# Three layer norm roots per row: from ScalarE's square root to GpSimd's power

## The reference, cut to what matters

```python
def _layernorm(x, axis=-1, eps=1e-05):
    m = jnp.mean(x, axis=axis, keepdims=True); v = jnp.var(x, axis=axis, keepdims=True)
    return (x - m) / jnp.sqrt(v + eps)
x = _layernorm(x + L0_attention(x))       # differential attention, 16 heads of 8
x = _layernorm(x + L0_ffn(x))             # gate, up, down with 4 bit blocks
x = _layernorm(x + L1_attention(x))       # 16 query heads, 4 key heads, causal
x = _layernorm(x + L1_ffn(x))             # eight experts, each token to one of them
```

## Time and profile before

| what | value |
|---|---|
| median of 3 runs (lowest, highest) | 1262.83 us (1258.26, 1266.27) |
| the profiled execution: its time, its span | 1266.14 us, 1264.3 us |
| mean granted TensorE clock in it | 0.843 of full |
| PE, DVE, ACT, POOL busy | 81%, 62%, 51%, 34% of the span |
| instructions | 20021 |

### The profile page before, as it was taken

How to read it: one execution, slowest core, us unless ns; L and a number is a source line. 1 busy time by engine, 2 the same in 40 slices (tenths; PEclk the granted TensorE clock), 3 DMA queues, 4 the chain that set the end, 5 groups by cost and what they waited for, 6 DMA issues and landing times.

```text
span 1264.3 us, 20021 instructions
## 1 busy us (share of the span) xinstructions
PE 1021.1 (81%) x7121; PEld 520.7 (41%) x7121; DVE 786.8 (62%) x1785; ACT 641.5 (51%) x1581; POOL 424.9 (34%) x512
## 2 busy tenths in 40 slices
PE   2588846889999878999988887999988847998754
PEld 1122321233455332455445442355444447455544
DVE  4789347983777678760787667862577562467431
ACT  1177612776266344677167434686257514257423
POOL 3000020300776304000776502200485630487411
PEclk7578955899999875799999775799999968999957
DMA  5300063000013000320103000230100005100052
GB/s 154 96 3 3 10 184 59 2 2 11 0 35 76 1 2 9 125 86 10 31 26 93 1 1 2 83 106 32 32 1 10 1 6 209 32 1 10 1 192 63
DMA packets 54305, 56.83 MB, mean 45 GB/s; under 512 B 13688, under 2 KB 46016, under 8 KB 53440
## 3 DMA queue, kind: packets, MB, share of 16 engines
q1 hardware_dynamic: 53184, 53.47, 14.3%
q0 software_dynamic: 1024, 2.10, 0.6%
HBM read 43.16 MB, written 16.20 MB: 47 GB/s over the span
## 4 chain that ended last, share of the span: by engine, by line
PE 50%; DVE 21%; ACT 10%; issue 8%; POOL 4%; DMA 4%; SPq 3%; POOLq 0%; ACTq 0%; DVEq 0%
PE ps L1583 8%; DVE mx L969 8%; PE ps L1566 5%; PE ps L1612 5%; PE ps L1625 5%; PE ps L1645 4%; PE ps L1655 4%; PE ps L1404 3%; PE ps L1500 3%; ACT PROB L1261 2%; PE ps L1415 2%; PE ps L1398 2%; PE ps L1541 2%; ACT PROB L1303 2%; DMA qst<-mrow 2%
## 5 line engine op out<-in xcount | busy, mean ns | idle before, releaser
L969 DVE TENSOR_REDUCE mx<-ps 128x1 f32<-128x512 f32 x512 | 323.7, 684 | 90.3 <-PE ps L1541 88.1
L1261 ACT ACTIVATE PROB<-ps 128x512 f32<-128x512 f32 x512 | 276.6, 602 | 166.1 <-PE ps L1566 164.4
L577 POOL TENSOR_SCALAR PROB<-PROB,rsum 128x128 f32<-128x128 f32 (+3 forms) x224 | 229.8, 1038 | 72.4 <-DVE rsum L1102 72.0
L1303 ACT ACTIVATE PROB<-ps,mx 128x128 f32<-128x128 f32 (+3 forms) x256 | 133.1, 527 | 165.6 <-DVE mx L1097 163.9
L1583 PE MATMUL ps<-PROB,v 128*32 128x256 f32 x2048 | 184.2, 452 | 3.0 <-ACT OREG L1270 2.6
L1541 PE MATMUL ps<-kst,qst 24*128 24x512 bf16 x512 | 158.9, 477 | 34.1 <-DVE mx L969 26.6
L1566 PE MATMUL ps<-qst,kst 27*128 27x512 bf16 x512 | 142.3, 450 | 39.3 <-ACT PROB L1261 22.8
L558 POOL CAST mparts<-mx 128x16 bf16<-128x16 f32 x32 | 7.0, 218 | 449.4 <-DVE mx L969 427.1
L1097 DVE TENSOR_REDUCE mx<-ps 128x1 f32<-128x128 f32 (+3 forms) x256 | 113.0, 483 | 64.4 <-PE ps L1628 64.2
L1645 PE MATMUL ps<-cst,PROB 128*128 128x128 f32 x640 | 114.2, 298 | 38.5 <-ACT PROB L1318 13.5
L1625 PE MATMUL ps<-MREG,QREG 64*128 64x384 f32 (+3 forms) x512 | 106.9, 495 | 0.0
(11 more groups left out here) (217 smaller groups left out, 1379.6 us busy)
## 6 DMA issues: line engine op xcount, KB each, us to landing
wexp<-expert_rows SPq DMA_DIRECT2D x44, 514.0 KB, 5.2
qk_terms<-RREG SPq DMA_DIRECT2D x48, 128.0 KB, 2.1
kst<-qk_terms SPq DMA_DIRECT2D x16, 192.0 KB
qst<-qk_terms SPq DMA_DIRECT2D x16, 192.0 KB
RREG<-sorted_x SPq DMA_DIRECT2D x4, 704.0 KB, 4.7
sorted_y<-RREG SPq DMA_DIRECT2D x4, 704.0 KB, 3.9
expert_rows<-in_L_ffn_W_dram SPq DMA_DIRECT2D x1, 2048.0 KB
expert_rows<-in_L_ffn_W_dram SPq DMA_DIRECT2D x4, 512.0 KB
```

What stands on the lines that cost most here:

```text
L577: pool.tensor_scalar(tile, tile, rsum1[:, 2 * v + half:2 * v + half + 1], None, ALU.mult).then_inc(scaled1, 1)
L969: dve.tensor_reduce(mx0[:, ga % 2, col:col + 1], ps[:, max_bank(k, MAX_SLOT[n]), :], AX, ALU.max, negate=True).then_inc(slot0_free, 1)
L1261: act.activation(prob0[:, s % 2, q % 4, q % 8 // 4], ps[:, s0_banks[q % len(s0_banks)], :], ACT.Exp, scale=float(HD0) ** -0.5).then_inc(ex ...
L1303: act.activation(prob1[:, half, at:at + w], ps[:, a1_bank(v, half), 0:w], ACT.Exp, bias=mx1[:, col:col + 1], accum_out=sum1[:, col:col + 1 ...
```

## The change

The second, third and fourth root of a row leave ACT. POOL adds the epsilon and raises the sum to the power -0.5 (a `tensor_tensor` with a 128x4 tile filled with -0.5), which gives the reciprocal root at once. POOL also makes `var2`. So ACT loses three square roots a row, DVE loses three reciprocals and the two products of `both_scales`, and POOL gains two operations (`root_b`) and seven (`roots_c`), with new semaphores `rootB` and `rootC`. `roots_c` stands in POOL's list behind `max_parts0` of group 1 and ahead of that of group 2; `root_b` stands behind `max_parts0` of group 6. The first and the fifth root of a row stay on ACT, in `attention1`. No transfer is moved.

```diff
+            pool.memset(minus_half, -0.5).then_inc(setup_pool, 1)
...
+            def root_b(r):
+                pool.wait_ge(varB, 2 * r + 2)
+                step(pool.tensor_scalar(stB[:, 0], mvB[:, :, 1], LN_EPS, None, ALU.add)); settle()
+                pool.tensor_tensor(stB[:, 1], stB[:, 0], minus_half, ALU.pow).then_inc(rootB, 1)
+
+            def roots_c(i):
+                pool.wait_ge(varC, 2 * i + 1)
+                step(pool.tensor_scalar(stC[:, 0], mvC[:, :, 1], LN_EPS, None, ALU.add)); settle()
+                pool.tensor_tensor(stC[:, 1], stC[:, 0], minus_half, ALU.pow).then_inc(rootC, 1)
+                pool.wait_ge(rootC, 2 * i + 1)
+                step(pool.tensor_tensor(var2, mvC[:, :, 1], stC[:, 1], ALU.mult)); settle()
+                step(pool.tensor_tensor(var2, var2, stC[:, 1], ALU.mult)); settle()
+                step(pool.tensor_scalar(var2, var2, LN_EPS, None, ALU.add)); settle()
+                pool.tensor_tensor(inv2, var2, minus_half, ALU.pow).then_inc(rootC, 1)
...
                     if k < BATCH:
                         max_parts0(k, g)
+                    if 0 <= i and g == 1:
+                        roots_c(i)
+                    if hidden and g == 6:
+                        root_b(r)
...
-            def both_scales(i):
-                dve.wait_ge(stdC, 3 * i + 1)
-                step(dve.reciprocal(stC[:, 1], stC[:, 0])); settle()
-                step(dve.tensor_tensor(var2, mvC[:, :, 1], stC[:, 1], ALU.mult)); settle()
-                dve.tensor_tensor(var2, var2, stC[:, 1], ALU.mult).then_inc(varC, 1)
...
-                if (s, c) == (1, 2):
-                    both_scales(i)
                 if (s, c) == (1, 3):
+                    dve.wait_ge(rootC, 2 * i + 1)
...
                 if (s, c) == (2, 1):
-                    dve.wait_ge(stdC, 3 * i + 2)
-                    step(dve.reciprocal(inv2, stC[:, 0])); settle()
+                    dve.wait_ge(rootC, 2 * i + 2)
...
                 if (s, c) == (12, 1):
-                    scale(ZB, X, mvB, stB, stdB, 2 * r + 2, lnB)
+                    dve.wait_ge(rootB, r + 1)
...
-                if (s, c) == (1, 1):
-                    std_c(3 * i + 1)
-                    act.wait_ge(varC, 3 * i + 2)
-                    act.activation(stC[:, 0], var2, ACT.Sqrt, bias=eps[:, 0:1]).then_inc(stdC, 1)
...
-                if (s, c) == (11, 1):
-                    std_b(2 * r + 2)
```

## The result

The changed kernel took 1257.01 us (median of 22 runs, 1248.61 to 1264.69) against 1265.94 us for the kernel before (22 runs, 1258.26 to 1270.69); the ratio is 0.9938, 95% interval 0.9924 to 0.9953. By the ratio that is 7.9 us off, by the two medians 8.9; forecast were 13.2 us off and 1249.6 us. Where a run's ratio stands, the us off given with it are by the ratio too. In two later comparisons with a fresh set of runs of the kernel before the ratio was 0.9901 [0.9872, 0.9930] and 0.9928 [0.9906, 0.9949], 12.6 and 9.1 us off. So the direction holds and the size was too large, also over all three.

The account below looks back on a forecast made before the run. No engine is full; waits around the roots bound the kernel, ACT standing between exponentials. Terms 7.9 - 0.4 + 5.8 + 0.4 - 0.5 = 13.2 us off give 1249.6 us from the median; range 1240 to 1268, forecast's own 1243 to 1256.

Parts of the forecast that it names:

- The pair in overlaps 1 and 2: Second and third root: without ACT's wait and table loads DVE's next maxima start 3.94 us sooner per overlap, 7.9 us gained.
- the table loads stay: Rival: loads are put elsewhere and stay; only the wait for the second variance goes, 1.6 us twice; 1260 us, chance 0.04.
- The feed-forward root: In overlaps 1 and 2: 1.4 us from lost table loads and 1.5 us from the clock not falling, each; 5.8 us gained.
- Contention: POOL's power slows DVE's 128x704 scaling behind the pair's variances in overlaps 1 and 2; 0.2 us each, 0.4 us lost.
- Overlap(0) at 0: Feed-forward root of overlap(0): ACT's reload came after its wait for PE and delays no PE work, so 0 us gained.
- the maximum rows' transfers: Behind overlap(1)'s pair, transfers are wanted 3.9 us sooner, leaving 1.8 us to land; only more time would cut the gain.
- The late roots: Overlaps 3 and 4: 0.4 us gained from a table load in overlap(3), 0.5 us charged for POOL's chain in both.
- p: Time of one POOL power on 128x4, priced by no profile row; taken as 0.6 us, with ends 0.2 and 3.2 us.
- under 1 us: Sign to look for in the profile: POOL's powers take less than 1 us each by their spacing.
- half is given back: Rival: clock still falls at the feed-forward stretch and PE or DVE wait behind the pairs; 6.5 us less, 1256, chance 0.11.
- The clock rises sooner: Rival: behind overlap(1)'s pair a shorter stall lets PE's clock rise; up to 7 us less in two overlaps, 1236, chance 0.07.
- The long power: Rival: POOL's power delays the second roots; slower by 1% from about 4.3 us a power, 1293 at 8 us; chance 0.13.

Follow-up runs that it names:

- e6: Kernel before with only the second root of the pair in overlaps 1 and 2 moved to POOL; ratio 0.9954 to the kernel before.
- e5: Changed kernel plus unread square roots on ACT at the old places in overlaps 1 and 2, so table loads stay without the wait; ratio 0.9944 to before.
- e3: Kernel before with only the pairs of overlaps 1 to 4 on POOL, feed-forward roots on ACT; ratio 0.9919 to the kernel before.
- e8: Kernel before with only the feed-forward root of overlap(0) on POOL; ratio 0.9990 to the kernel before.
- e1: The changed kernel run again without edit, for a second profile; ratio 0.9901 to the kernel before.
- e7: Changed kernel with every POOL power taken twice, the first result unused; ratio 0.9952 to the kernel before.
- e9: Changed kernel with both roots of each pair in one 128x8 power, DVE preparing both variances in four instructions; ratio 0.9906 to the kernel before.
- e12: The changed kernel run once more without edit; ratio 0.9928 to the kernel before.
- e10: Kernel before with only the pairs of overlaps 3 and 4 on POOL; ratio 0.9988 to the kernel before.
- e14: Kernel before with the pairs of overlaps 3 and 4 and the feed-forward root of overlap(3) on POOL; ratio 1.0013 to the kernel before.
- e15: Changed kernel with only the roots of overlaps 0 to 2 on POOL, those of 3 and 4 on ACT; ratio 0.9879 to the kernel before.
- e11: Changed kernel with the pairs of overlaps 3 and 4 and overlap(0)'s feed-forward root back on ACT, second measurement; ratio 0.9890 to the kernel before.
- e2: Changed kernel with the pairs of overlaps 3 and 4 and overlap(0)'s feed-forward root back on ACT, first measurement; ratio 0.9896 to the kernel before.

## Why the prediction was right and wrong

*The pair in overlaps 1 and 2 (7.9 forecast): right, 8.4 measured.* The mechanism stated as well, a wait of ACT for DVE's second variance with exponentials behind it (e6). But the loads were taken for part of it, and in the rival "the table loads stay" the wait alone was priced at 1.6 us twice. e5 gives it all 4.2 twice: that price was wrong, the loads are covered there.

*The feed-forward root (5.8 forecast): right in size, 5.5 measured, and half right in one cause.* The loads cost 1.43 (1.4 forecast) and the clock 1.2 to 1.3 (1.5 forecast). The fall of the clock, however, was put down to PE's wait for ACT just ahead of it. Without that wait it stayed away every time, as forecast; but with the wait in place it stayed away in five of six stretches once the pair's stall was gone too (e3, e5, e6). The prediction did not have the stall as a condition. As either change mostly removes the fall, the gains of the two parts do not simply add.

*Contention (0.4 forecast): not seen on DVE.* Its scaling of 128x704 took 0.87 us in overlap(1) as before. POOL gave way (0.62 for 0.20 us), where it had time to, and in overlap(3) POOL's powers lengthened while DVE's 128x704 kept its 0.87 to 0.89 us. At the roots it was POOL that paid, where in the earlier trace rows DVE had. The rule of the Trainium skill that the prediction cites ("GPSIMD Engine Reference", Specifications) names the shared resource; the traces agree with that.

*Overlap(0) at 0, and the maximum rows' transfers:* not contradicted. e8 is within 0.1% of no change, though the profiles leave some 1.5 us in doubt there; in overlap(1) the maxima after the pair wait for PE no more than before (0.75 and 0.76 us).

*The late roots (0.4 - 0.5 forecast): the step that failed.* "For the two last overlaps I charge 0.5 us" rests on p = 0.6, and p was 1.04 to 1.05, or up to 1.85 beside DVE; the second root pays for it twice. The sign "under 1 us" failed with it. By the prediction's own chain, 1.3 + 2p, a p of 1.04 puts the second root 3.4 us behind the variances; in overlap(4) it is there after 3.6. DVE waits 0.94 + 0.93 and 1.49 + 0.98 us for the pairs, and 1.5 us for the feed-forward root of overlap(3), where under 0.5 was forecast; that last stage is 0.64 us shorter all the same, since ACT's load is gone (0.4 forecast). The pairs cost 1.1 us in overlap(3) and 2.1 in overlap(4), 3.2 where 0.5 was charged; with the 0.64 gained, 2.5 where 0.1 was charged. For overlap(3) the prediction held that other work of DVE's stands ahead, so that the root can hardly cost more; it does stand there, but beside it POOL's own operations grew longer.

In overlap(4) 1.0 is the chain: the copy behind the product with the second root starts 4.19 us behind the variances, where it was 3.16 (before, then after):

```profile
1203.13 0.69 DVE L867 COPY XQ<-ps 128x512 f32<-128x512 f32 x1 [0.40 <-PE ps L1393]
```

```profile
1198.79 0.68 DVE L881 COPY XQ<-ps 128x512 f32<-128x512 f32 x1
```

The rest goes with the clock, which is still low when the experts' products run: 25.4 us behind the centring, 10 us of before and then of after (the clock is again the last number but two):

```profile
1225.00:1235.00 10.00, 10.00 (x77) 10.00 (x77) 0.00 (x0) 6.44 (x23) 0.00 (x0) 0.83 0.97 361
```

```profile
1219.60:1229.60 10.00, 9.23 (x56) 9.08 (x56) 0.72 (x2) 4.71 (x17) 0.00 (x0) 0.65 0.90 349
```

In this stretch the six profiles with all of these roots on POOL (after, e1, e5, e7, e9, e12) were granted 0.65 to 0.70, and overlap(4) took 61.8 to 62.8 us; the other eleven were granted 0.78 to 0.83, also the three with these pairs on POOL (e3, e10, e14: 60.3 to 60.9 us).

*"From the median 1249.6":* the median then was of three runs, 1262.83; over 22 it is 1265.94. Of the 7.4 us between 1249.6 and 1257.0 these are 3.1. The other 4.3 are the 13.2 forecast less the 8.9 by the medians. The stages give some 12, 1.2 less than forecast: the late roots cost 2.4 more than charged, and the other stages gave 1.2 more. The 3.1 that remain of these 4.3 are in no stage of the sum; up to 1.5 of them may lie behind the feed-forward root of overlap(0), which e8 does not confirm.

*The rivals.* The median lies at 1257.0, just above the forecast's own range and next to the rival "half is given back" (1256). That nearness is luck: the clock did not fall at the feed-forward root, and DVE's wait behind the pair of overlap(1) did not grow. "The clock rises sooner" did not come: behind the pair of overlap(1) the stretch got no shorter. The long power was out by its condition: p stayed below 2.5.

Open: the 3.1 us that no stage holds, and why overlap(4) meets the lower clock only with the whole change. That is 1 to 2 us which the late half costs together with the early half and not by itself. The executions of one kernel differ by 8 to 16 us where there are ten or more, and over the 22 runs of the changed kernel time and granted clock go together (correlation -0.86), so the last microseconds cannot be placed.

The lowest ratios are those of the two versions that keep the pairs of overlaps 3 and 4 on ACT: 0.9879 (e15), 0.9890 and 0.9896 (e11 and e2); the changed kernel's 0.9901 lies within their intervals.

## What to carry to other kernels

Moving a small serial step to an idle engine pays where work stands queued behind it on the old engine, and costs the latency that it adds where the consumer has nothing else to do; decide it for each place, not for the operation. When an engine waits in the middle of its list, look for the one operation that makes it wait: here moving one of two roots shortened that stretch as much as moving both. Take a second profile of the kernel before, and a median of more than three runs, before a difference of 5 us in 1260 is read stage by stage.

## What was not expected of the hardware

- A GpSimd power of 128x4 takes 1.04 us, of 128x8 1.67 us, and the same of 128x4 up to 1.85 us beside VectorE's 128x704 operations, while the products and adds of 128x4 take 0.20 to 0.23 us in overlap(1), and one product 0.62 us beside such an operation. The first power, in overlap(0), starts 0.09 us after the add ahead of it and takes 1.05 us like the others: the pause of some 6 us that the Trainium skill ("GPSIMD Engine Reference", Instruction dispatch) gives to the first call of a freshly loaded routine does not show here; whether the power is such a routine, no run shows.
- The granted clock in a stretch takes different courses in executions of one kernel: 69.5 us with 0.72 and then 1.00, 74.2 us with 0.53 and then 0.76, for the same stage of the kernel before.
- With PE, DVE and ACT busy alike in the 7 us ahead (5.31, 4.26 and 6.94 us), the clock fell to 0.76 in the kernel before and in e3's overlap(1), and stayed at 1.00 in e6. What PE did just ahead does not settle it; the fall was rarer, one of six against ten of ten, where the pair's stall some 85 us earlier was gone.
